# Adaptive-weights FFN with top-1 routing: fp32 routing in four column groups, per batch of eight tiles

## What is computed

```
h    = x[b] @ W[cat[b]] + bias[cat[b]]            # 4096 x 512, fp32
prob = softmax(h @ Wr)                            # 8 experts
e    = argmax(prob);  rank = tokens of e before this one
keep = rank < 512                                 # capacity of an expert
y    = prob[e] * (relu(h @ W1[e]) @ W2[e])        # only where keep
out  = x + y                                      # a dropped token gives x
```

## Time and profile before

| | us |
|---|---|
| median of 3 runs | 873.74 |
| lowest, highest | 871.19, 875.33 |
| profiled execution | 873.38 |
| its span, first to last instruction | 871.7 |
| PE busy in the span | 850.4 |
| DVE, ACT, POOL busy | 426.7, 257.4, 205.8 |
| mean granted TensorE clock | 0.983 |

### The profile page before, as it was taken

How to read it: one execution, slowest core, us unless ns; L and a number is a source line. 1 busy time by engine, 2 the same in 40 slices (tenths; PEclk the granted TensorE clock), 3 DMA queues, 4 the chain that set the end, 5 groups by cost and what they waited for, 6 DMA issues and landing times.

```text
span 871.7 us, 10460 instructions
## 1 busy us (share of the span) xinstructions
PE 850.4 (98%) x3952; PEld 690.1 (79%) x3953; DVE 426.7 (49%) x640; ACT 257.4 (30%) x361; POOL 205.8 (24%) x205
## 2 busy tenths in 40 slices
PE   8999999799999999999999999999999999999994
PEld 5777777588888888888888888888888888888883
DVE  4586677236343634363436343634363436343632
ACT  3322211223222322232223222322232223222320
POOL 1000000730730073007300731073007300030001
PEclk9898999999999999999999999999999999999997
DMA  8784755732444244424342444244424432242001
GB/s 295 294 316 163 281 204 234 232 128 97 140 151 147 97 140 151 144 98 143 141 145 97 139 150 144 98 137 151 147 97 138 157 135 96 99 152 94 0 0 48
DMA packets 54201, 126.86 MB, mean 146 GB/s; under 512 B 5752, under 2 KB 5752, under 8 KB 53538
## 3 DMA queue, kind: packets, MB, share of 16 engines
q1 hardware_dynamic: 42674, 93.35, 31.1%
q0 software_dynamic: 10928, 32.16, 10.4%
q10 hardware_dynamic: 576, 1.05, 0.4%
HBM read 110.13 MB, written 25.17 MB: 155 GB/s over the span
## 4 chain that ended last, share of the span: by engine, by line
PE 94%; DMA 2%; SPq 1%; DVE 1%; issue 1%; POOL 0%; ACT 0%; POOLq 0%; DVEq 0%
PE acc_ps L843 40%; PE y_ps L826 40%; PE acc_ps L759 7%; PE tp_ps L759 3%; PE tp_ps L705 2%; PE y_ps L690 2%; DMA b_col<-cond_b 1%; DMA rows<-h_rows,tok_all 1%; PE y_ps L738 0%; POOL out L360 0%; SPq L244 0%; PE y_ps L714 0%; DVE rows L507 0%; DVE rows L674 0%; SPq L213 0%
## 5 line engine op out<-in xcount | busy, mean ns | idle before, releaser
L843 PE MATMUL acc_ps<-xt_split,w_split 128*128 128x512 f32 x1536 | 367.8, 389 | 1.1 <-DVE xt_split L627 1.1
L826 PE MATMUL y_ps<-w_split,xt_split 128*128 128x512 f32 x1536 | 367.6, 389 | 0.0
L843 PEld LDWEIGHTS acc_ps<-xt_split,w_split 128*128 128x128 f32 x1536 | 288.2, 188 | 61.1 <-DVE xt_split L627 1.2
L826 PEld LDWEIGHTS y_ps<-w_split,xt_split 128*128 128x128 f32 x1536 | 288.3, 188 | 59.8
L651 DVE SCALAR_TENSOR_TENSOR xt_split<-acc_ps,xt_split 128x512 fp32r<-128x512 f32 x128 | 88.6, 692 | 314.7 <-ACT xt_split L456 314.7
L456 ACT ACTIVATE xt_split<-acc_ps 128x512 fp32r<-128x512 f32 x128 | 76.5, 598 | 401.6 <-PE acc_ps L843 401.6
L335 POOL DMA_INDIRECT rows<-h_rows,idx_all x112 | 122.8, 1097 | 265.5 <-DVE tp_ps L641 233.0
L568 DVE TENSOR_TENSOR w_split<-stage,w_split 128x1024 fp32r<-128x1024 f32 x66 | 80.9, 1226 | 19.3 <-ACT w_split L407 19.3
L574 DVE TENSOR_TENSOR w_split<-stage,w_split 128x1024 fp32r<-128x1024 f32 x66 | 80.9, 1226 | 16.4 <-ACT w_split L413 16.4
L360 POOL DMA_INDIRECT out<-rows,put_all x32 | 32.0, 999 | 222.8 <-DVE rows L674 217.6
L759 PE MATMUL acc_ps<-w_split,xt_split 128*128 128x512 f32 x264 | 70.8, 422 | 1.0 <-DVE w_split L487 1.0
(11 more groups left out here) (85 smaller groups left out, 258.2 us busy)
## 6 DMA issues: line engine op xcount, KB each, us to landing
stage<-w SPq DMA_DIRECT2D x64, 1024.0 KB, 5.3
stage<-x_t SPq DMA_DIRECT2D x7, 1024.0 KB, 8.0
h_rows<-rows POOLq DMA_DIRECT2D x7, 1024.0 KB, 8.2
stage<-cond_wt SPq DMA_DIRECT2D x4, 1024.0 KB, 7.8
stage<-cond_w SPq DMA_DIRECT2D x3, 1024.0 KB, 6.4
rows<-h_rows,idx_all POOLq DMA_INDIRECT x112
stage<-x_t ACTq DMA_DIRECT2D x4, 256.0 KB, 3.4
stage<-cond_w SPq DMA_DIRECT2D x4, 256.0 KB, 3.0
```

The source lines that it names most:

```text
L826: last = nc.tensor.matmul(y_ps[:, s, :], hts[:, j % 2, a, s * P:(s + 1) * P], w2s[:, slot, w, kk, :], start=(j == 0 and (a, w) == (HI, HI) ...
L843: last = nc.tensor.matmul(acc_ps[:, j % 2, :], w1s[:, slot, w, k, jj * P:(jj + 1) * P], xts[:, par, a, k, :], start=(k == 0 and (w, a) == ...
```

## The change

The routing works on a whole batch (8 tiles, TPB) instead of a chunk, and in plain fp32 instead of split parts.

- `m_turn(b)` takes the place of `m_product(b)`. The padded router weights (32 columns, `wr32`) are the stationary operand and the block of transposed conditioning weights streams as 512 columns. Each of the four blocks k of the sum writes its own 32 rows of one PSUM bank (`turn_ps`), and nothing is accumulated; the bias does the same. ACT copies the bank to SBUF (`copy_turned`), and `m_sum(b)` adds the four groups by four fp32 matmuls against `fold`, a matrix of ones and zeros. DVE copies the result (`copy_m`).
- `route(c)` is four fp32 matmuls of 512 columns, one for each k and group of rows, straight from the raw x^T. `by_token(b)` adds the groups and turns them to token order in one: 8 fp32 matmuls against `fold`.
- `choose`, `rank_of`, `place`, `fill_table` do 8 tiles at a time, four times instead of eight.
- The raw x^T stays until its route is done, so it has four slots: stage slots 2 and 3 and two more (`x_more`), which lie in the memory that half of w1_split uses later. ACT and DVE split x in halves of a chunk (1024 columns) instead of quarters.
- `copy_x` is gone. For each expert number e, SP loads 512 rows of x (1 MB) into the memory of the bias rows, and POOL writes them to `out` by index in four indirect DMAs; the index of a row whose token has a slot lies past the end, and such a row isn't written. SP waits for the writes before it reloads the memory.
- On DVE the wait for all masks now stands ahead of the first split of x, with the making of `fold`.

The diff, cut to the lists, the loads, the copy of x and PE's new steps (`choose`, `place`, `rank_of` and `fill_table` differ only in their width):

```diff
-    ROUTE = [3, 5, 7, 9] + [TPC * (c - 1) for c in range(4, NCH)]
-    CHOOSE = [n + 1 for n in ROUTE]
-    PLACE = [n + 2 for n in ROUTE]
-    FILL = [n + 4 for n in ROUTE]
-    PRODUCT = [ROUTE[CPB * b] - (2 if b > 1 else 1) for b in range(BATCH)]
-    SPLIT_X = [None, (1, 1, 2, 2), (4, 4, 5, 5), (6, 6, 7, 7)] + [range(TPC * (c - 2), TPC * (c - 1)) for c in range(4, NCH)]
-    SPLIT_W = [None, (4, 5, 6, 6)] + [tuple(2 * TPC * (b - 1) + n for n in (1, 3, 3, 4)) for b in range(2, BATCH)]
...
+    M_TURN = [1, 6, 11, 17]
+    M_SUM = [2, 7, 12, 18]
+    ROUTE = [3, 4, 8, 9, 13, 15, 19, 21]
+    CHOOSE = [5, 10, 16, 22]
+    PLACE = [6, 11, 18, 24]
+    FILL = [8, 13, 20, 26]
+    SPLIT_X = [None, (1, 2), (4, 5), (6, 7)] + [(TPC * (c - 2), TPC * (c - 2) + 2) for c in range(4, NCH)]
+    SPLIT_W = [None, (4, 5, 6, 6)] + [tuple(2 * TPC * (b - 1) + n for n in (1, 3, 3, 5)) for b in range(2, BATCH)]
...
+        with nc.sbuf_tensor("x_more", [P, 2, DK, CH], f32) as x_more:
+            pass
...
+        x_in = [stage[:, 2, :, :], stage[:, 3, :, :], x_more[:, 0, :, :], x_more[:, 1, :, :]]
...
+            def load_next_xt(c):
+                sp.wait_ge(s_xlo, DK + 2 * (c - 4))
+                sp.wait_ge(s_lt, c - 3)
+                load_xt(c)
+            load_xt(2)
+            sp.wait_ge(s_wlo, DK)
+            sp.dma_start(stage[:, 1, :, :], cond_view(1)).then_inc(s_stage[1], 16)
+            load_xt(3)
+            sp.wait_ge(s_turn, 1)
+            load_cond_wt(1)
+            load_bias_rows(1)
+            for b in range(2, BATCH):
+                load_next_xt(CPB * b)
+                load_next_xt(CPB * b + 1)
+                sp.wait_ge(s_turn, b)
+                load_cond_wt(b)
                 sp.wait_ge(s_wlo, DK * b)
                 sp.dma_start(stage[:, 1, :, :], cond_view(b)).then_inc(s_stage[1], 16)
-                sp.wait_ge(s_m, b)
-                load_cond_wt(b)
-                sp.wait_ge(s_xlo, DK * CPB * b)
-                load_xt(CPB * b + 1)
                 load_bias_rows(b)
-                copy_x(b)
...
+            def load_x_rows(e):
+                sp.dma_start(b_rows[:, :, :], x_v[:, bass.ds(e, 1), :, :].rearrange("p o t d -> p (o t) d")
+                             ).then_inc(s_xrow, 16)
...
             with sp.Fori(0, E - 1) as e:
+                sp.wait_ge(s_drop, e * (16 * BATCH))
+                load_x_rows(e)
                 for q in range(QN):
...
+                pool.wait_ge(s_xrow, 16 * (e + 1))
+                for t in range(BATCH):
+                    pool.indirect_dma_start(
+                        out=out, out_offset=bass.IndirectOffsetOnAxis(ap=drop_all[:, BATCH * e + t:BATCH * e + t + 1],
+                                                                      axis=0),
+                        in_=b_rows[:, t, :], in_offset=None,
+                        bounds_check=TOKENS - 1, oob_is_err=False).then_inc(s_drop, 16)
...
+            def copy_turned(b):
+                act.wait_ge(s_turn, b + 1)
+                if b >= 1:
+                    act.wait_ge(s_lg, b)
+                nc.scalar.activation(logits_t[:, 1, :], turn_ps, ACTF.Copy).then_inc(s_turnc, 1)
...
+                then(nc.vector.scalar_tensor_tensor(drop_f[:, :], payload[:, :, 0], float(P), payload[:, :, 1],
+                                                    ALU.mult, ALU.add))
+                then(nc.vector.tensor_scalar(place_all[:, :], place_all[:, :], float(CAP), float(SKIP),
+                                             ALU.is_lt, ALU.mult))
+                then(nc.vector.tensor_tensor(drop_f[:, :], drop_f[:, :], place_all[:, :], ALU.add))
+                then(nc.vector.tensor_copy(drop_all[:, :], drop_f[:, :]))
...
-            def m_product(b):
+            def m_turn(b):
                 pe.wait_ge(s_stage[0], 16 * (b + 1))
                 if b == 0:
                     pe.wait_ge(s_const, 16 * (BATCH + 1))
+                    pe.wait_ge(s_wr0, 2)
                 else:
-                    pe.wait_ge(s_msplit, b)
+                    pe.wait_ge(s_ltc, CPB * b)
+                    pe.wait_ge(s_mcopy, b)
+                for k in range(DK):
+                    nc.tensor.matmul(turn_ps[k * G:(k + 1) * G, :], wr32[:, k, :], stage[:, 0, k, :],
+                                     start=True, stop=True)
+                for k in range(DK):
+                    last = nc.tensor.matmul(bias_ps[k * G:(k + 1) * G, :], wr32[:, k, :], b_col[:, b, k:k + 1],
+                                            start=True, stop=True)
+                last.then_inc(s_turn, 1)
+            def m_sum(b):
+                pe.wait_ge(s_turnc, b + 1)
+                if b == 0:
+                    pe.wait_ge(s_fold, 1)
                 for m in range(DK):
-                    for k in range(DK):
-                        nc.tensor.matmul(m_ps[:, m, :], stage[:, 0, k, m * P:(m + 1) * P], wr16[:, k, 0:E],
-                                         start=(k == 0), stop=(k == DK - 1))
-                for k in range(DK):
-                    last = nc.tensor.matmul(bias_ps, wr16[:, k, :], b_col[:, b, k:k + 1],
-                                            start=(k == 0), stop=(k == DK - 1))
+                    last = nc.tensor.matmul(m_ps[:, m, :], logits_t[:, 1, m * P:(m + 1) * P], fold[:, :],
+                                            start=True, stop=True)
                 last.then_inc(s_m, 1)
             def route(c):
-                pe.wait_ge(s_msplit, c // CPB + 1)
-                pe.wait_ge(s_xlo, DK * (c + 1))
+                pe.wait_ge(s_mcopy, c // CPB + 1)
                 if c >= 1:
+                    pe.wait_ge(s_xin[c % 4], 16 * (c // 4 + (c % 4 > 0)))
+                if c % CPB:
                     pe.wait_ge(s_ltc, c)
                 for k in range(DK):
-                    for part in (HI, LO):
-                        last = nc.tensor.matmul(tp_ps[0:16, 0, :], m_split[:, k, :], xts[:, c % 4, part, k, :],
-                                                start=(k == 0 and part == HI), stop=(k == DK - 1 and part == LO))
+                    last = nc.tensor.matmul(turn_ps[k * G:(k + 1) * G, :], m32[:, (c // CPB) % 2, k, :],
+                                            x_in[c % 4][:, k, :], start=True, stop=True)
                 last.then_inc(s_lt, 1)
-            def by_token(c):
-                pe.wait_ge(s_ltc, c + 1)
-                if c >= 1:
-                    pe.wait_ge(s_oh, c)
-                for t in range(TPC):
-                    last = nc.tensor.transpose(tok_ps[:, t, :], logits_t[:, c % 2, t * P:(t + 1) * P],
-                                               ident[0:16, 0:16])
+            def by_token(b):
+                pe.wait_ge(s_ltc, CPB * (b + 1))
+                if b >= 1:
+                    pe.wait_ge(s_oh, b)
+                for t in range(TPB):
+                    last = nc.tensor.matmul(tok_ps[:, t, :], logits_t[:, t // TPC, (t % TPC) * P:(t % TPC + 1) * P],
+                                            fold[:, :], start=True, stop=True)
                 last.then_inc(s_lg, 1)
```

286 lines of the change are left out of this document (152 added, 134 removed).

## The result

The changed kernel takes 898.33 us, the median of 4 runs (894.63 to 901.09), against 873.36 us for the kernel before on the same chip. The ratio is 1.028, with a 95% interval of 1.026 to 1.030: it is slower by 2.8%. The prediction said 871.5 us with a range of 854 to 882. It was wrong by 27 us, and the time lies outside the range.

The account below looks back on a forecast made before the run. The prediction took PE's own queue to bound the kernel, full in routing and experts. From 873.38 us, less 4.9 for routing, plus 2.9 at the start, it got 871.4 and said 871.5 us, range 854 to 882.

Parts of the forecast that it names:

- Cost 0: Expert stage: the x-row loads and indirect writes fit into idle time and add 0, at most 3 us.
- the experts at 696 us: Sign to look for in the profile after: the expert stage stays at 696 us.
- The fourth rival: Experts: copies not hidden, POOL or SP late by 0.5 to 1 us each, 875 to 880 us; chance 0.03.
- The end is unchanged: End of the program: the change adds no time there.
- PE starts matmuls strictly in the order of its queue: Column groups: only neighbours overlap, so a call takes five steps of 0.427 us, 2.13 us; twelve calls 25.6 us.
- The first rival: Column groups: all four run fully side by side, 0.85 us a call, 856 us in total; chance 0.30.
- rival 2: Column groups: no overlap for fp32, 3.41 us a call, 887 us in total; chance 0.15.
- Does DVE become the bound? 0: Routing: DVE's larger batches still let store_h come back in time, cost 0, at worst 4 x 0.5 us.
- The start: Routing's start: first m_turn, now ahead of tile 2, waits for small loads, so PE idles; + 2.9 us.
- rival 3: Clock falls anyway, behind by_token or the new idle at the start; 879.7 us if four slow tiles stay; chance 0.10.
- the 8.25 us of slow tiles: Routing: extra time of four low-clock tiles behind the old matrix product, counted as gone: 8.25 us saved.
- The routing's sum: Routing stage: new work 37.2 us against 42.1 removed, a gain of 4.9 us, less 2.9 us at the start.

Follow-up runs that it names:

- e2_small_pad: Changed kernel with 20 more instructions on PE ahead of the expert loop (zero matmuls, about the same columns streamed): 874.62 us.
- e1_pad: Changed kernel with 84 more instructions on PE ahead of the expert loop (more, narrower zero matmuls): 882.28 us, ratio 0.999 to the kernel before.
- e6_pad_again: e1_pad run again on another chip beside more runs of the kernel before: 882.59 us, ratio 1.004.
- e8_serial: e1_pad with a route call's four matmuls accumulating in the same 32 PSUM rows instead of four groups; routing results not right: 901.16 us.
- e7_best: e1_pad with first m_turn behind tile 2, copy_m right behind store_h, and x rows loaded behind two weight loads: 874.35 us, ratio 0.988 to the kernel before.
- e10_best_copyx: e7_best's routing with the old DRAM to DRAM copies of x, no x rows in the experts: 852.74 us, ratio 0.976 to the kernel before.
- e3_copyx: Changed kernel with the old four 2 MB copies of x, no x rows in the experts, PE's instructions untouched: 892.55 us.
- e4_before_shift: Kernel before with 176 more instructions on PE ahead of the expert loop (zero matmuls): 896.24 us.
- e5_far_pad: Changed kernel with 226 more instructions on PE ahead of the expert loop (zero matmuls): 894.28 us.

## Why the prediction was wrong

**No term for the place of the loop: +31.6 us.** The step that failed is "Cost 0" for the experts, with "the experts at 696 us" as its sign: they took 728.2. The prediction costs every edit by what it does, not by how many instructions stand ahead of a loop. The page of the kernel before could have warned: 13 packets in q8 for a program with three backward branches means that the body is held in the engine's memory. This was no rival either. The fourth rival has the copies late by 0.5 to 1 us in each expert, not a burst of loads at a branch; if the rows of x lengthen the stalls, that part is some 4 us of each 10.5. With the stalls undone, the stages of the first chip give 873.38 - 8.3 - 1.4 + 3.5 = 867.2 us, an estimate that no run reached: e2_small_pad took 874.62 once, and e1_pad and e6_pad_again 882.3 and 882.6 with 12 to 14 us lost in the first expert. Where that comes near the 871.5 of the forecast, it is luck: the errors named next partly cancel.

**"The end is unchanged": +3.5 us.** It follows the writes of x rows, shown by seven kernels with and seven without; the forecast gave no reason for it.

**The column groups: the step "PE starts matmuls strictly in the order of its queue" failed.** I took 2.13 us for a call; it is 1.06. Twelve calls would cost 12.7 us, not 25.6. The first rival's mechanism was the right one and its 0.85 us was near: two steps of 0.427, and 0.2 more. e8_serial's 3.62 confirms the price of a column (3.41 from above) and so the bound of rival 2. The Trainium skill (TensorE: Matmul & The Clock Gate, Part 3) has overlap of column groups; this trace agrees with that, and not with five steps that I drew from its words on order: four records start together, and then the other four. Changes between tiles and groups cost little, as was assumed: the tile between two calls takes 2.95 us from start to start (29.47 to 32.42), where an ordinary one takes 2.82.

**"Does DVE become the bound? 0": 4.4 us of idle and more.** The waits of PE between 18 and 139 us in the changed kernel:

```profile
PE tp_ps L771 <- DVE bias_g L544: 4.4, 3, 2.9
PE tp_ps L746 <- issue: 2.4, 1, 2.4
```

I had asked whether store_h comes back in time, but the operation that PE waits for is copy_m. It stands right behind place on DVE in the fourth batch (2.94 us of wait), and behind place, a store_h and a split of x in the second and third (1.23 and 0.26 us). DVE's timeline (the eight selects took 2.19 us, as the earlier trace rows doubled; place from 93.93 to 98.42):

```profile
95.03 0.18 DVE L594 TENSOR_TENSOR payload<-rest,payload 128x8 bf16<-128x8 f32 x1
95.25 0.56 DVE L597 TENSOR_TENSOR packed<-onehot,payload 128x384 bf16<-128x384 bf16 x1
...
96.23 2.19 DVE L607 TENSOR_SCALAR select<-iota_c,place_all 128x512 bf16<-128x512 f16 x8
98.34 0.19 DVE L543 COPY m<-y_ps 128x32 f32<-128x32 f32 x1
```

And on PE, with the clock down behind the wait:

```profile
98.64 1.94 PE L771 MATMUL tp_ps<-x_more,m 128*32 128x512 f32 x8 [2.94 <-DVE bias_g L544]
100.51 3.67 PE L827 MATMUL tp_ps<-w_split,xt_split 128*128 128x512 f32 x12
```

The size of place was right (4.6 us forecast, 4.5 measured). What failed was to look for one consumer of DVE only.

**The start: right, and with a part of rival 3.** PE stands idle for 2.44 us at 19.29, where 2.9 was forecast, and the tile behind is slow: 4.30 us where the next takes 2.98.

```profile
19.29 1.34 PE L746 MATMUL tp_ps<-stage,wr 128*32 128x512 f32 x8 [2.44 <-issue]
20.33 0.36 PE L749 MATMUL y_ps<-b_col,wr 128*32 128x1 f32 x8
20.62 4.30 PE L827 MATMUL tp_ps<-w_split,xt_split 128*128 128x512 f32 x12
24.75 0.96 PE L759 MATMUL y_ps<-fold,logits_t 128*128 128x8 f32 x8
25.57 2.98 PE L827 MATMUL acc_ps<-w_split,xt_split 128*128 128x512 f32 x12
```

e7_best and e10_best_copyx took away both idle stretches and the slow tiles with them: 10.5 us.

**What came as forecast.** The stage's clock rose from 0.92 to 0.97 with the product of 8 columns gone, so the 8.25 us of slow tiles are real. m_sum costs 0.8 us a batch (3.5 in all forecast, 3.3 measured); no tile behind by_token is slow. The copies are hidden within the experts, if perhaps not at the branches: the first two are full, and POOL's idle ahead of the first output write went from 10.99 us to 5.53, where 6 was said:

```profile
240.06 0.98 POOL L394 DMA_INDIRECT out<-rows,put_all  x1 [5.53 <-DVE rows L729]
...
251.03 1.04 POOL L356 DMA_INDIRECT rows<-x,tok_all  x1 [6.15 <-DMA out<-rows,put_all]
```

The output writes land late behind SP's loads, and the gather of x waits 6.15 us for them, which nothing on the path needs.

**The routing's sum.** Forecast -2.0 us (-4.9 + 2.9). With calls at 1.06 us it would be 12.9 lower, -14.9; the idle for copy_m gives 4.4 back, and the slow calls and tiles behind the idle stretches (1.34, 4.30, 1.94 and 3.67 against 1.06, 2.98, 1.06 and 3.01) give 3.1: -7.4, measured -8.3.

## What to carry to other kernels

Where an engine loops over a long body (about 1,597 instructions on PE here), the number of instructions ahead of the loop can be a cost of its own: read the instruction queue's packets before and after a change, and where they rise, move the loop by a few instructions before judging the change. For an engine that is full, follow every operation that it waits for on its helpers, not the one that was nearest to late before. A stage that improves can stand inside a kernel that gets slower, so split the spans by stage before looking for a reason in the edited code.

## What the hardware showed that I had not expected

- One or two waits, the longest of them 3.6 to 4.8 us, and slow matmuls behind them at each backward branch, 10.5 us together in the changed kernel and 6.0 to 7.8 us in e3_copyx, e4_before_shift and e5_far_pad, at the places of the loop that fit eight blocks; 0.5 us at most at the places that fit seven.
- Four fp32 matmuls of 512 columns in four column groups take 1.06 us, in one group 3.62 us: a factor of 3.4.
- In the changed kernel's routing, idle stretches of 2.4 and 2.9 us were each followed by a tile at the lower clock, while the 1.23 us at 51.15 was not (3.01 us for the tile behind).
- With the indirect writes of x rows and their loads in the experts the end is 3.5 us longer, though the last output writes land as before.
- On two of four chips the entry of the experts cost 1.9 to 15.7 us more, with and without rows of x, and for the kernel before as far as its times tell; its cause is open.
